# Two-layer graph network: per-edge gate scores and per-node totals put into separate 32-column groups of TensorE

## The reference

```python
# layer 0
msgs = z[edge_dst] @ Wd + z[edge_src] @ Ws + edge_weight[:, None] * ww + bm
agg  = where(deg > 0, segment_max(msgs, edge_dst), 0)
x    = layernorm(x + relu(z @ W1a + agg @ W1b + b1) @ W2 + b2)
# layer 1
h  = x @ node_fc_W + node_fc_b
he = edge_features @ edge_fc_W + edge_fc_b
a  = sum(h[src] * h[dst], axis=-1)
t  = relu(einsum('ed,mdf->emf', he, rel_att_W1) + rel_att_b1)     # m = 0, 1, 2
g  = sigmoid(einsum('emf,mf->em', t, rel_att_W2) + rel_att_b2)    # a gate per edge and relation
alpha, beta = seg_softmax(a, dst), seg_softmax(g, dst)
h_att = segment_sum(alpha * einsum('ed,kdf->ef', h[src], node_att_W), dst) / 3
h_rel = segment_sum(einsum('em,emf->ef', beta, einsum('ed,mdf->emf', h[src], rel_att_W)), dst) / 3
h_red = relu(concat([h_att, h_rel]) @ out_fc_W + out_fc_b)
x = layernorm(x + gate * where(deg > 0, h_red, h) + (1 - gate) * x)
```

## Time and profile before

| | us |
|---|---|
| time, median of 3 runs | 2290.52 |
| the 3 runs | 2287.78, 2290.52, 2296.37 |
| span of the profiled execution, first to last instruction | 2723.8 |
| PE busy in it | 1843.7 |
| POOL busy in it | 1639.6 |
| DVE busy in it | 1328.7 |
| ACT busy in it | 1115.3 |
| mean granted PE clock in it | 0.806 of full |

### The profile page before, as it was taken

One profiled execution on the slowest core, in us unless ns is written; L12 is line 12 of the kernel. 1 busy time (PEld: TensorE's weight loads), 2 busy tenths in 40 slices (PEclk: granted clock), 3 DMA queues, 4 the chain that ended last, 5 costly groups with the idle time before them and its releaser, 6 DMA issues. The chain is left out here.

```text
span 2723.8 us, 43235 instructions
## 1 busy us (share of the span) xinstructions
PE 1843.7 (68%) x9891; PEld 1146.6 (42%) x9891; DVE 1328.7 (49%) x5220; ACT 1115.3 (41%) x3305; POOL 1639.6 (60%) x1705
## 2 busy tenths in 40 slices
PE   4577777677767777655666766676776776766665
PEld 3122222222222222114355655565665665655565
DVE  3454555554444444324535544544544545445459
ACT  1233333333333333333544444444444444444448
POOL 3666666666767777646455655555565655555525
PEclk7689888888889888876867777777777777777788
DMA  8433333333333333323311221221112221211113
GB/s 228 144 120 124 109 116 118 125 109 109 121 109 114 101 123 110 124 80 87 116 46 47 54 51 48 52 51 49 51 51 50 53 52 49 52 48 50 49 44 119
DMA packets 115983, 235.04 MB, mean 86 GB/s; under 512 B 32909, under 2 KB 68230, under 8 KB 106422
## 3 DMA queue, kind: packets, MB, share of 16 engines
q0 software_dynamic: 52832, 109.39, 16.3%
q1 hardware_dynamic: 56522, 97.21, 9.7%
q10 hardware_dynamic: 6540, 27.42, 2.9%
HBM read 166.01 MB, written 67.89 MB: 86 GB/s over the span
## 5 line engine op out<-in xcount | busy, mean ns | idle before, releaser
L463 POOL DMA_INDIRECT d_region<-d_h,d_region x784 | 747.8, 954 | 534.2 <-issue 221.1
L209 POOL DMA_INDIRECT acc<-d_src_product,b_region x784 | 779.4, 994 | 378.6 <-issue 225.5
L651 PE MATMUL banks<-acc,b_region 64*128 64x512 f32 x1176 | 351.8, 706 | 213.9 <-ACT acc L756 99.4
L859 DVE SCALAR_TENSOR_TENSOR acc<-b_region,acc 128x128 f32<-128x128 f32 x784 | 271.4, 346 | 433.6 <-DMA acc<-d_src_product,b_region 416.8
L1577 DVE TENSOR_TENSOR acc<-acc,banks 128x160 f32 x784 | 252.5, 322 | 318.6 <-remote 124.0
L1376 PE MATMUL banks<-d_region 128*128 128x128 f32 x1568 | 306.0, 357 | 4.1 <-issue 3.8
L1379 PE MATMUL banks<-d_region,pick 128*128 128x128 f32 x1568 | 294.1, 346 | 11.6 <-issue 11.2
L651 PEld LDWEIGHTS banks<-acc,b_region 64*128 64x128 f32 x1176 | 109.8, 211 | 429.7 <-issue 188.3
L1379 PEld LDWEIGHTS banks<-d_region,pick 128*128 128x128 f32 x1568 | 277.4, 262 | 13.6 <-issue 13.4
L1376 PEld LDWEIGHTS banks<-d_region 128*128 128x128 f32 x1568 | 271.2, 260 | 10.3 <-issue 5.3
L870 DVE SCALAR_TENSOR_TENSOR acc<-acc,b_region 128x128 f32<-128x128 f32 x784 | 270.1, 345 | 7.5 <-remote 5.2
(11 more groups left out here) (261 smaller groups left out, 2450.3 us busy)
## 6 DMA issues: line engine op xcount, KB each, us to landing
d_runs<-acc SPq DMA_DIRECT2D x48, 1024.0 KB
acc<-ea ACTq DMA_DIRECT2D x25, 1024.0 KB
acc<-d_src_product,b_region POOLq DMA_INDIRECT x784
d_region<-d_h,d_region POOLq DMA_INDIRECT x784
d_region<-d_rel SPq DMA_DIRECT2D x49, 256.0 KB
hT<-xT SPq DMA_DIRECT2D x7, 448.0 KB, 6.9
d_src_product<-acc SPq DMA_DIRECT2D x7, 448.0 KB, 3.7
acc<-xrow SPq DMA_DIRECT2D x1, 3136.0 KB
```

What stands on the lines that cost most here:

```text
L209: pool.indirect_dma_start(self.rows[:, s, j, :], None, d["B"], bass.IndirectOffsetOnAxis(self.idx[:, k:k + 1], 0)).then_inc(self.gathered[ ...
L463: pool.indirect_dma_start(rows[:, s, :], None, table, bass.IndirectOffsetOnAxis(idx[:, s:s + 1], 0)).then_inc(gathered[q], 16)
L651: last = nc.tensor.matmul(bank[4 + n % 2 * 2 + h][:, :], wf[h * DE:(h + 1) * DE, m * P:(m + 1) * P], ea[h * DE:(h + 1) * DE, u % (2 * UC), ...
L859: nc.vector.scalar_tensor_tensor(rows[:, s, j, :], wwb, wgt[:, k:k + 1], rows[:, s, j, :], ALU.mult, ALU.add).then_inc(ch, 1)
```

## The change

Three things change together.

- `dots`: the three relations go to three column groups (PSUM rows 0, 32 and 64 on), and the two halves add up inside each. `w2m` is 99 columns wide instead of 96, with the weights of relation m in column 33m + 1; a block that begins one column earlier or later puts them in its column 0 or 1, so half h is row h of each group. ACT copies 96 rows instead of 64, and the store takes every 32nd row.
- totals of the edge pass: `pick` is replaced by `one`, a single column of ones, read 32 times over. Total k is a product of its own in column group k, and stands in all 32 rows of it. `rescale` scales 32 rows instead of one.
- `turn_sums`: the totals now stand in rows 0, 32, 64 and 96, so the transposes of 4 rows become products of all 128 rows with four columns of the identity.

```diff
-    t["pick"] = sb("pick", [P, P + M])
+    t["one"] = sb("one", [P, 1])
...
-            c.add(nc.gpsimd.memset(t["pick"][:, :], 0.0))
+            c.add(nc.gpsimd.memset(t["one"][:, :], 1.0))
...
-            c.add(nc.gpsimd.memset(t["pick"][:, M:M + 1], 1.0))
...
-        wf, w2m = ca(M * P), ca(M * W)
+        wf, w2m = ca(M * P), ca(M * (W + 1))
...
-                for m in range(M):
-                    for h in range(2):
-                        last = nc.tensor.matmul(bank[3][h * W:(h + 1) * W, :], w2m[:, m * W:(m + 1) * W],
-                                                rt[u % 2][m][:, h * G4:(h + 1) * G4], start=(m == 0), stop=(m == M - 1))
+                for h in range(2):
+                    for m in range(M):
+                        col = m * (W + 1) + 1 - h
+                        last = nc.tensor.matmul(bank[3][m * W:(m + 1) * W, :], w2m[:, col:col + W],
+                                                rt[u % 2][m][:, h * G4:(h + 1) * G4], start=(h == 0), stop=(h == 1))
...
-                    act.dma_start(to[h], gout[u % 2][h * W:h * W + M, :].rearrange("m (t e) -> m t e", t=GJ)
+                    act.dma_start(to[h], gout[u % 2][h:h + (M - 1) * W + 1:W, :].rearrange("m (t e) -> m t e", t=GJ)
...
-                    nc.scalar.activation(gout[u % 2][0:2 * W, :], bank[3][0:2 * W, :], ACT.Copy).then_inc(gc, 1)
+                    nc.scalar.activation(gout[u % 2][0:M * W, :], bank[3][0:M * W, :], ACT.Copy).then_inc(gc, 1)
...
-            c.add(nc.vector.tensor_copy(w2m[:, 0:M * W:W + 1], w2))
+            c.add(nc.vector.tensor_copy(w2m[:, 1:M * (W + 1):W + 1], w2))
...
                 for k in range(1 + M):
-                    last = nc.tensor.matmul(Z[q % 2], pick[:, M - k:M - k + P], wts[q % 2][:, :, k, :],
-                                            start=(k == 0), stop=(k == M))
+                    last = nc.tensor.matmul(Z[q % 2][k * W:(k + 1) * W, :], one[:, 0:1].to_broadcast([P, W]),
+                                            wts[q % 2][:, :, k, :], start=True, stop=True)
...
-                w = acc[0:1, 4, bass.ds(base[0], 1)]
-                nc.scalar.activation(w, w, ACT.Copy, scale=fac[q % 4][0:1, :]).then_inc(res, 1)
+                w = acc[0:W, 4, bass.ds(base[0], 1)]
+                nc.scalar.activation(w, w, ACT.Copy, scale=fac[q % 4][0:W, :]).then_inc(res, 1)
...
-                    last = nc.tensor.transpose(to[:, K * b:K * (b + 1)], acc[0:K, 4, b * P:(b + 1) * P], ident[0:K, 0:K])
+                    last = nc.tensor.matmul(to[:, K * b:K * (b + 1)], acc[:, 4, b * P:(b + 1) * P], ident[:, 0:P:W],
+                                            start=True, stop=True)
```

More of the change, by code:

```diff
@@ L270, in _ @@
                                  allow_small_or_imprecise_dtypes=True))
-            c.add(nc.gpsimd.memset(t["pick"][:, M:M + 1], 1.0))
-            assert c.n == 11
+            assert c.n == 10
             pool.wait_ge(stt, 16)
@@ L337, in _ @@
             c.add(nc.vector.memset(kcum[:, 0:1], 0.0))
-            dve.wait_ge(cst, 11)
+            dve.wait_ge(cst, 10)
             c.add(nc.vector.tensor_tensor_scan(kcum[:, 1:TC], ones[:, 0:TC - 1], km[:, 0:TC - 1], 0.0,
@@ L383, in _ @@
         def _(pe):
-            pe.wait_ge(cst, 11)
+            pe.wait_ge(cst, 10)
             def product(c):
@@ L1249, in phase_edges @@
         TURNED, SCORES, WEIGHTS, BOUNDS = bank[0], bank[1], bank[2], bank[3]
-        ident, pick = t["ident"], t["pick"]
+        ident, one = t["ident"], t["one"]
         acc = t["acc"]
```

## The result

The changed kernel takes 2305.22 us (median of 4 runs, 2304.56 to 2305.71), the kernel before 2289.15 in the runs beside it (2287.2 to 2296.37). The ratio is 1.0075, interval [1.0055, 1.0095]: slower by 17.2 us, with an interval from 12.6 to 21.7. The likeliest case was put at 2293 to 2303 in one place, which ends just under it, and at 2290 to 2306 in another, which just holds it. No change within 0.5% had the largest chance, 0.50; slower by more than that, which came, had 0.30.

What follows compares the result with a forecast made beforehand. POOL's gathers were taken to set the pace of both long phases. The turning's +12.0 us and -2.5 us at the start and end of the edge pass gave +9.5 on 2290.5: 2300 us, range 2240 to 2312.

Steps and rivals of the forecast that it cites:

- The likeliest case: Whole kernel: POOL sets the pace and the clock falls within the turning of the totals; 2293 to 2303 us, chance 0.58.
- POOL's pace: Both long phases run at the pace of POOL's gathers, 1.25 us each; two times 980 and 318 make 2278 us.
- The first rival: Edge pass: PE and DVE set the pace, so PE's saving shows; 2246 us, or 2192 with all of it; chance 0.13.
- the third: Edge pass: the clock falls since PE idles more; a body takes 4.6 us, under POOL's 5.0; time unchanged, no chance given.
- Totals side by side: Edge pass: the new four products save 0.55 us a body at the higher clock, 1.12 at the lower; hidden by POOL.
- the last rival: Edge pass: the four totals do not run side by side, L1379 keeps about 0.9 us; 2303 us, no chance given.
- Dots: Runs phase: 4 rounds instead of 6 save 0.9 to 1.5 us of PE a unit, hidden by POOL; costed at nothing.
- Start of the edge pass: POOL waits for PE's sixth group, and the first body's faster totals lie ahead of that: -1.1 us.
- End of the edge pass: After the last gather five bodies are left, half of 0.55 us saved in each: -1.4 us.
- The turning: Start of the last phase, L1698: float32 products replace 49 transposes with nothing to hide them, clock falling half-way: +12.0 us.
- The second rival: Start of the last phase: the whole turning of the totals runs at the lower clock; +14.8 us, 2305 us, chance 0.17.
- the -2.5 for all else: Start and end of the edge pass together: -2.5 us, with bounds 0 and 108 us.

Runs made afterwards that it cites:

- the other profile: The kernel before, profiled once more with no edit: 2287.28 us.
- the doubled totals: The kernel before with the four products of the edge pass's totals issued twice: ratio 1.0003 [0.9989, 1.0016].
- the dense form: The changed kernel with the turning's four identity columns repeated to 128, held side by side in a tile of their own: 2293.97 us.

## Why the prediction was right or wrong

**POOL's pace: right, by a sum that fitted partly by luck.** The sum put 1.25 us a gather into the unprofiled runs; they are 1.27 apart in the edge pass of both kernels and 1.30 in the runs phase. With the 318 us outside the gathers, taken from the stretched profile, this fitted: the other profile has some 273 there and 2013 us of gathers, where the sum had 1960 to 1997, so two errors made up for each other. The conclusion stands on the runs: PE's 226 us left no trace in the time, and the doubled totals cost nothing. The first rival, PE and DVE as the pace, is out; the third, a lower clock in the edge pass at no cost, came about (0.88 to 0.79). That the 433 us were of that profile and not of the kernel was right too.

**Totals side by side: right in size.** The step of L1353 was taken for the new form; the profile has 0.43 us for either row. The saving was 142.6/196 = 0.73 us a body over all clocks, between the 0.55 and 1.12 forecast. The four do run side by side, so the last rival is out. The Trainium skill ("TensorEngine Tiling (Array Packing)", "Key Properties") has a change of tiling mode drain the engine. If that is what puts the totals 0.98 us behind the start of L1376's row in after (2157.11 to 2158.09) and 0.89 in the kernel before (1607.31 to 1608.20), at 1.06 us busy in both, it is 0.1 us for one change, and the sign did not turn.

**Dots: right.** 1.92 us a unit where 1.9 was named, saving 0.85 us; hidden.

**Start of the edge pass: wrong.** The step failed that took -1.1 us from POOL's 13.47 us of idle time at the sixth group. In the profile that isn't stretched no such wait exists: between its gathers POOL never stands for more than 0.31 us in the first eighty us of the pass, in both kernels. A wait was read off a profile that had been found stretched, and the text had said that such terms carry over.

**End of the edge pass: -1.4 forecast.** From the last gather's start to the end of the last addition 2194.55 - 2168.43 = 26.1 us passed before and 24.1 in after. Over all unstretched profiles the kernels with the new totals have 23.2 to 25.3 and those with the old ones 24.9 to 26.5: the sign and about the size are right.

**The turning: right, its clock by a choice.** +12.0 was forecast: 14.4 us for the 90 records at a clock that falls half-way, instead of 2.98, and +0.6 for the eight. In after they took 14.69, the clock fell about half-way, and the turning alone costs +12.6 (7.5 to 17.6). Half-way was chosen between two ends, with no row that said so; in two other profiles with four columns the clock fell sooner (16.75 and 16.86 us), so that 14.4 came so near owes something to luck. The second rival, the lower clock throughout, named 2305 us, which is the time measured, but that is a coincidence: the row is not the 18.9 us of that rival, and its clock is 1.00 for the first 36 records. The open question, what four moving columns do to the clock, is answered for this row: in the three profiles with four columns shown here the clock fell from 1.00 to 0.50 within the 90 records, and with 128 columns it stayed at 1.00 throughout the row. The Trainium skill ("TensorE: Matmul & The Clock Gate", Part 1) has the clock follow how busy PE was; by the profile's count this trace does not bear that out, since PE was busy 4.00 us in each 4.00 while the clock fell to 0.50.

One consequence was missed: the low clock outlasts the turning. In after, chunk 1's 32 records take 6.50 us; in the dense form they take 3.85 at the higher clock, and the stretch of the table is 6.2 us shorter than in after, 4.5 of it from the 90 records. Against the kernel before the loss is only 1.0 us, for there too the clock was down behind the turning (0.68 over 2203.70 to 2209.00) and chunk 1 took 5.48.

**The sum.** Forecast +9.5, measured +17.2 (12.6 to 21.7). The turning term is met; the step that failed is the -2.5 for all else, put on the start and the end of the edge pass, in whose place the kernel without the new turning has +4.3 (0.9 to 7.5), 6.8 us more. Of these 1.1 are the wait that did not exist. The two profiles of after and of the kernel before differ by 17.9 us in span: +5.5 ahead of the first gather of the edge pass, -0.3 in its gathers, -2.0 from the last gather to the last addition, +14.8 in the stretch of the table and -0.2 behind it. Within the stretch the turning itself has 12.3, chunk 0 has 1.5 and chunk 1 has 1.0. But neither the 5.5 nor chunk 0's 1.5 can be laid to the change: the run with the totals twice, whose code is that of the kernel before up to the edge pass, begins its gathers there 5.3 us later than the kernel before too (1177.81 against 1172.48), and chunk 0 varies by more with one code. The runs phase takes from its first to its last gather 1018.5 us in after and 1014.8 before, but 1014.3 to 1021.9 over all unstretched profiles. What makes up the rest of the 6.8 us stays open; the spread of single profiles is as large as the term.

## What to carry to other kernels

A saving on an engine is worth nothing while another sets the pace, and a few records added in a place where nothing covers them cost their full length: 226 us less of PE gave nothing, and 49 products in place of 49 small transposes cost 12.6 us. When a stretched profile is found, no wait of it should enter a sum, only durations of instructions. A float32 record with a 128x128 stationary block took 0.10 us with 4 moving columns and 0.11 with 128 dense ones here, both at the full clock, so the narrow form saved next to nothing; and the clock fell within the row of the narrow ones and not within that of the wide ones.

## What was not expected of the hardware

The same 90 records are faster with more columns: 10.21 us with 128 dense columns, at a granted clock of 1.00, against 14.69 to 16.86 with 4, where the clock fell to 0.50.

At the full clock 128 columns that are four, 32 words apart, read again and again take 0.222 us a record, dense ones 0.113.

Two profiles of the same program had spans of 2723.8 and 2285.5 us.
